# The four output products stand between the next group's two shared halves

## The reference

```python
shared = x2 @ sw1.T * _sqrelu(x2 @ swg.T) @ sw2.T      # hidden width 256
xl = x2 @ Wdown.T                                       # latent width 128
probas = jax.nn.sigmoid(x2 @ Wg.T)                      # 16 experts
_, idx = jax.lax.top_k(probas + biases, K)              # K = 8
...                                                     # w_dense from idx, p
for e in range(E):
    ye = xl @ rw1[e].T * _sqrelu(xl @ rwg[e].T) @ rw2[e].T
    acc = acc + w_dense[:, e:e + 1] * ye
out = shared + acc @ Wup.T
```

## Time and profile before

| | |
|---|---|
| median of three runs | 2818.55 us |
| profiled execution | 2816.09 us, span 2814.3 us |
| TensorE matmul busy | 2586.7 us (92%), granted clock 0.989 over the run |
| VectorE, ScalarE, GpSimd busy | 1937.4, 1816.8, 1199.5 us |
| DMA | 197.67 MB, mean 70 GB/s |

### The profile page before, as it was taken

How to read it: one execution, slowest core, us unless ns; L and a number is a source line. 1 busy time by engine, 2 the same in 40 slices (tenths; PEclk the granted TensorE clock), 3 DMA queues, 4 the chain that set the end, 5 groups by cost and what they waited for, 6 DMA issues and landing times.

```text
span 2814.3 us, 48768 instructions
## 1 busy us (share of the span) xinstructions
PE 2586.7 (92%) x13025; PEld 1862.8 (66%) x13120; DVE 1937.4 (69%) x3742; ACT 1816.8 (65%) x4597; POOL 1199.5 (43%) x1275
## 2 busy tenths in 40 slices
PE   3899999999999999679999999999999999999998
PEld 2566656666666666457777777777777777777776
DVE  4666666666666665486786686687677668668667
ACT  2666666666666667376675675676566567567566
POOL 3333333333333333044454464454445445446445
PEclk8999999999999999799999999999999999999999
DMA  3111111222211111343132122212213212221222
GB/s 104 24 61 60 60 60 60 65 66 64 64 60 60 60 45 59 103 120 99 38 98 83 53 82 83 80 48 90 80 40 94 83 46 89 83 68 63 87 67 58
DMA packets 99807, 197.67 MB, mean 70 GB/s; under 512 B 10928, under 2 KB 10928, under 8 KB 99568
## 3 DMA queue, kind: packets, MB, share of 16 engines
q1 hardware_dynamic: 94576, 179.29, 19.4%
q0 software_dynamic: 5120, 17.31, 2.8%
HBM read 128.89 MB, written 34.08 MB: 58 GB/s over the span
## 4 chain that ended last, share of the span: by engine, by line
issue 28%; POOL 26%; DVE 2%; PE 1%; ACT 1%; POOLq 1%; DMA 0%; SPq 0%; DVEq 0%; ACTq 0%
POOL t_lo L1127 24%; POOL sh_lo L1127 1%; DVE t L1494 1%; DVE t L1487 1%; POOLq L1125 0%; DVE f_lo L1512 0%; DMA x<-h 0%; ACT x L1286 0%; PE fwork L1142 0%; PE fwork L1143 0%; PE fwork L1144 0%; DMA w_rows<-wT 0%; PE fwork L1166 0%; DVE fxT_lo L1433 0%; PE ps_u L1142 0%
## 5 line engine op out<-in xcount | busy, mean ns | idle before, releaser
L1127 POOL TENSOR_TENSOR t_lo<-t,t_hi 128x512 fp32r<-128x512 f32 x512 | 738.2, 1452 | 469.8 <-ACT t_hi L1341 469.5
L1494 DVE TENSOR_TENSOR t<-t,w_all 128x512 f32<-128x512 f32 x512 | 605.5, 1183 | 35.7 <-DMA w_all<-w_rows 7.7
L377 POOL TENSOR_TENSOR probs<-probs,inv 128x512 f32<-128x512 f32 x256 | 265.0, 1041 | 626.8 <-DVE inv L774 626.6
L1487 DVE TENSOR_TENSOR t<-ps_u,square 128x512 f32<-128x512 f32 x544 | 372.3, 684 | 207.0 <-PE ps_u L1144 125.5
L599 ACT ACTIVATE probs<-ps_s,nmax 128x128 f32<-128x128 f32 x1024 | 362.5, 370 | 222.6 <-DVE nmax L769 222.6
L1341 ACT ACTIVATE t_hi<-t 128x512 fp32r<-128x512 f32 x512 | 320.6, 626 | 249.4 <-DVE t L1494 246.9
L1324 ACT ACTIVATE square<-ps_g 128x512 f32<-128x512 f32 x544 | 316.3, 581 | 91.3 <-PE ps_g L1144 89.3
L1328 ACT ACTIVATE square<-square 128x512 f32<-128x512 f32 x544 | 344.0, 632 | 17.3
L488 PE MATMUL ps_s<-k_diag,qT 128*128 128x512 f32 x512 | 263.9, 597 | 7.8 <-DVE qT L745 1.1
L1142 PE MATMUL ps_y<-t_hi,f_hi 128*128 128x512 f32 x512 | 227.3, 444 | 40.2 <-POOL t_lo L1127 39.3
L769 DVE TENSOR_REDUCE nmax<-ps_s 128x4 f32<-128x512 f32 x256 | 176.1, 688 | 102.2 <-PE ps_s L488 100.7
(11 more groups left out here) (195 smaller groups left out, 5449.4 us busy)
## 6 DMA issues: line engine op xcount, KB each, us to landing
w_all<-w_rows SPq DMA_DIRECT2D x256, 256.0 KB, 3.2
res_next<-h SPq DMA_DIRECT2D x64, 256.0 KB, 2.3
res<-res_next SPq DMA_DIRECT2D x64, 256.0 KB, 2.3
h<-res SPq DMA_DIRECT2D x64, 256.0 KB, 2.0
x<-h SPq DMA_DIRECT2D x16, 1024.0 KB, 6.0
fres<-h SPq DMA_DIRECT2D x16, 1024.0 KB, 7.6
out<-fres SPq DMA_DIRECT2D x64, 256.0 KB, 2.2
fres<-in_w_ffn SPq DMA_DIRECT2D x14, 512.0 KB, 3.7
```

The source lines that it names most:

```text
L377: pool.tensor_tensor(probs[:, s % 4, :, :], probs[:, s % 4, :, :], inv[:, s % 4, :].rearrange("p (h o) -> p h o", o=1).to_broadcast([P, HP ...
L1127: pool.tensor_tensor(lo, t[:, t_slot(j), :], hi.bitcast(F32), ALU.subtract).then_inc(t_lo_done, 1)
L1487: dve.tensor_tensor(t[:, t_slot(j), :], ps_u[:, j % 2, :], square[:, j % 2, :], ALU.mult).then_inc(t1_done, 1)
L1494: dve.tensor_tensor(t[:, t_slot(j), :], t[:, t_slot(j), :], w_all[:, e % 2, :], ALU.mult).then_inc(t_done, 1)
```

## The change

On TensorE, the second shared half of group g + 1 moves behind the four outputs of group g; the first half and `weights_turn` stay ahead of them. VectorE and ScalarE are reordered to follow: `linear(g+1, 0)` stands behind the first `add_out`, `linear(g+1, 1)` behind the last one; `weights_copy` moves ahead of `squares_end(g+1, 0)`, and both `hidden_hi` of the shared halves stand ahead of the next group (before, the second stood behind the next group's first expert square). GpSimd and SyncE are not edited.

```diff
@@ TensorE, group() @@
                 if more:
                     logits_turn(g + 1, half)
                     shared(g + 1, 0)
-                    shared(g + 1, 1)
                     weights_turn(g + 1, half)
                 for i in range(TILES):
                     output(g, out_half(g), i)
+                if more:
+                    shared(g + 1, 1)
@@ ScalarE, group() @@
                     squares_end(g, HC + n)
-                    hidden_hi(g, HC + n - 1)
+                    if n > 0:
+                        hidden_hi(g, HC + n - 1)
...
                     squares(g + 1, 0)
+                    weights_copy(g + 1, half)
                     squares_end(g + 1, 0)
+                    hidden_hi(g + 1, 0)
                     squares(g + 1, 1)
                     squares_end(g + 1, 1)
-                    weights_copy(g + 1, half)
-                    hidden_hi(g + 1, 0)
+                    hidden_hi(g + 1, 1)
@@ ScalarE, ahead of group 0 @@
             weights_copy(0, 0)
             hidden_hi(0, 0)
+            hidden_hi(0, 1)
             group(0, True)
@@ VectorE, group() @@
                 if more:
                     routing(g + 1, half)
-                    linear(g + 1, 0)
-                    linear(g + 1, 1)
                 for i in range(TILES):
                     add_out(g, i)
+                    if more and i == 0:
+                        linear(g + 1, 0)
+                if more:
+                    linear(g + 1, 1)
```

## The result

The changed kernel takes 2863.99 us (median of 4 runs, 2859.52 to 2865.10) against 2818.09 us for the kernel before (4 runs, 2815.90 to 2821.38). The ratio is 1.0159, 95% interval 1.0141 to 1.0177. The prediction, 2830.4 us with a range up to 2846, had the sign and the mechanism, but only a quarter of the size (11.9 us forecast, 45.9 measured); the time lies outside the range of 2809 to 2846.

The account below looks back on a forecast made before the run. VectorE's wait for its own code at the loop's 13 jumps was taken to end TensorE's border wait. 13 x (0.06 + 0.9) - 0.6 = +11.9 us on the median 2818.55 gave 2830.4 us, range 2809 to 2846.

Parts of the forecast that it names:

- T: Time mark at the group border: end of the last matmul ahead of the new group's first expert product.
- The +0.06 us of the later `linear`: VectorE before its branch: `linear(g+1, 1)` starts 0.09 us after its matmul, against 0.03 for `add_out`; +0.06 us per border.
- the border out of the loop: Border without a jump on leaving the loop: first `ps_y` 0.3 us sooner, counted twice with the entry, 0.6 us gained.
- the prologue: Ahead of group 0: `hidden_hi(0, 1)` moves there, hidden by the first `weigh`'s 6.10 us wait for weights; costs nothing.
- X: Extra time of VectorE's code fetch at each of 13 jumps beside a full DMA queue: 0.9 us, bounds 0 to 3.0.
- B: Rival: VectorE's loop top stays resident after the reordering, branch 0.3 us instead of 2.8; 10.1 us gained, 2808.4 us; chance 0.14.
- nothing queued behind `linear` is new: VectorE ahead of its branch: the `linear` replacing the last `add_out` has nothing new queued behind it; only +0.06 us per border.
- A shift of a few instructions seldom crosses a block: Argument against ScalarE's branch beginning to miss when its code ahead of the loop grows by a few instructions.
- X reaches TensorE in full: Chain `linear`, `weigh`, ScalarE, GpSimd, `ps_y`: the fetch's extra 0.9 us per jump delays TensorE in full, none returned later.
- A: Rival: VectorE's code fetch isn't slowed by the full DMA queue, extra time near 0; +0.2 us, 2818.7 us; chance 0.27.
- C: Rival: VectorE's code fetch slowed by 2 to 3 us per jump; +26.2 to +39.2 us, 2844.7 to 2857.7 us; chance 0.09.
- D: Rival: ScalarE's loop branch begins to miss, its top 2.5 us later; +24.1 us, 2842.7 us; chance 0.04.

Follow-up runs that it names:

- b_early_x: Kernel before, only SyncE's list changed: stores of output tiles 2 and 3 moved behind the next x load, which issues earlier; 2860.06 us, ratio 1.0136.
- a_extra_load: Changed kernel with one more 1 MB transfer issued by SyncE behind each residual load; 2871.94 us, ratio 1.0184.
- a_late_x: Changed kernel with SyncE's next x and residual loads issued only after VectorE's unit 0 linear, behind its jump; 2850.11 us, ratio 1.0098.
- a_shift64: Changed kernel with 64 more sequencer instructions ahead of VectorE's feed-forward loop; 2809.61 us, ratio 0.9957, and 2814.93 us, ratio 0.9979, when measured again.
- a_shift8_late: Changed kernel with 8 more sequencer instructions ahead of VectorE's loop and SyncE's x and residual loads behind its jump; 2837.02 us, ratio 1.0056.
- a_shift8: Changed kernel with 8 more sequencer instructions ahead of VectorE's feed-forward loop; 2852.50 us, ratio 1.0113.

## Why the prediction was wrong

*What bounds, and where the change acts: right.* The jump of VectorE's loop sets the border, and the change acts through SyncE's loads, which no line of the diff touches. The loads came at the predicted T - 3.3 and T - 2.3; TensorE didn't stand at `weights_turn` or at the outputs; ScalarE stayed hidden at the jumps; unit 0's Square ended at T + 2.66 where the sum had 2.64. At the border out of the loop the first `ps_y` came 0.3 us sooner, as in the sum, but at the one into it only 0.2 us (T + 6.95 instead of 7.13): the sum took the exit for both. The +0.06 us of the later `linear` is there, and the prologue cost nothing that a row shows.

*X: the term that failed.* I put 0.9 us per jump on the slowed fetch, with 3.0 as the upper end; it measured 3.6 (6.49 - 2.88). Two errors lie in it.

First, the load's part. It is 2.9 to 3.0 us, just what I had called the upper bound: if the packet in the earlier trace rows was asked for as soon as VectorE went on at T + 3.0, it needed up to 3.9 us instead of 0.9. I set this reading aside for the scatter of that packet, 0.75 us above its earliest. But a scatter tells only how a delay varies, not how large its fixed part is. b_early_x shows that the reading was right: its code lies as in the kernel before, the jump ends later, and when VectorE goes on the load has all but gone (DMA share 0.22 from 1420.5 to 1422.0). There the same packet comes 0.6 to 0.9 us behind the loop's top; in the kernel before it comes 2.6 to 3.9 us behind it, 3.2 on average. The instruction queue of b_early_x's first turn, from 1421.3 to 1421.8 us, with its loop top at 1420.6:

```profile
q14 instruction: 1, 0.01, 3.8%
```

b_early_x and a_extra_load show a large fixed part too: no first packet came sooner than 3.6 us behind T, against 1.1 in the kernel before. The estimate of 0.7 us from the Trainium skill ("DMA: Bandwidth & Descriptors", "Queues, rings and completion order", on arbitration) points the same way as the measurement and is four times too small.

Second, the other fetch, which I left out: 0.6 to 0.7 us in series, and 0.35 us at the crossing. The trace had it. A code packet came about 2 us ahead of every jump, and I used it in rival B only. The step "nothing queued behind `linear` is new" counted instructions, and not what entering the next block of code asks for. "A shift of a few instructions seldom crosses a block" was true of ScalarE; VectorE's loop, as the fetches and shifts place it, already stood with its end 2 or 3 instructions behind a boundary, so what stands last in the loop decides when the boundary is crossed.

*The chain into TensorE: nearly right.* "X reaches TensorE in full" holds to some 0.7 us: unit 0's `linear` came 4.0 us later against T (3.6 and 0.35 and 0.06), the first `ps_y` 4.4 us later, and the turn grew by 3.71 us. Between `linear` and `ps_y` it takes 4.5 us instead of 4.1, with TensorE at its lower clock behind the longer stop (a_late_x, where the clock stays at 1.00 behind all jumps but one, has 4.1). This was not in the sum.

*The rivals.* A fell at once (it needed an unchanged branch). C was the case that came true, in its main mechanism and nearly in place: its upper end of 2857.7 us is 6 us short, and it had 0.09. Its bound for the load was right; the second fetch was in no rival. B, with its loop top resident, didn't happen by the change, but its border is what a_shift64 built: 0.3 us per jump and 2809.61 us, against 2808.4 worked out for B (2814.93 in the second measurement). D didn't occur: ScalarE's branch took 0.24 us at every jump.

## What to carry to other kernels

When a loop's back edge is on the critical path, read the sequencer's branch and the next instruction at the top, engine by engine, and the instruction packets beside them: a few instructions more or fewer ahead of the loop can be worth more than a reordering of its work. When a change moves an engine's results, follow the DMA queue that waits for them and ask what the transfers now fall on; code fetches use the same engines. Take a delay that no row shows from the longest consistent reading of the nearest row and not from that row's scatter, until an experiment decides.

## What the runs showed of the hardware

- A jump of VectorE's loop cost 2.8 to 2.9 us with a fetch of code and light DMA load (before, a_shift8_late), 5.8 to 6.2 us with the DMA engines full (a_shift8, b_early_x), and 0.3 us without a fetch (the five runs with 64 or 120 more instructions).
- A fetch ahead that was asked for just before added 0.6 to 0.7 us in series (a_shift8 against the changed kernel, a_shift8_late against a_late_x).
- The loop of 275 instructions fetched its top at one offset and at 8 more, and kept it at 64 and at 120 more. This fits blocks of 128 instructions, with three of them kept and four not.
- Full DMA engines delayed the packet by about the same 3 us, with 2 MB of loads issued (6.49 us) or 3 MB (6.69 us).
- In the changed kernel, after some 4.5 us without a matmul, TensorE's granted clock fell from 1.00 to its 1.2 GHz level for 3.4 us in the first turn; the 0.6 us stops of the kernel before left it at 1.00.
